# A transformer block with routed experts on one core: the experts' tiles begin at slot 5 of the last batch's step instead of slot 9

## The reference

```python
mod = (_silu(L0_c) @ L0_wmod).reshape(16, 6, 1, -1)
sa, ca, ga, sb, cb, gb = (mod[:, 0], ..., mod[:, 5])     # gates: |g| at least 0.25, sign kept
h = _layernorm(x) * (1 + ca) + sa
x = x + ga * attention(h)          # 16 heads of 8, rotary, causal, softmax, output projection
h = _layernorm(x) * (1 + cb) + sb
x = x + gb * ffn(h)
# ffn: logits = h @ router_w.T over 8 experts, the best 2 of each token, weights renormalised
#      expert e: gelu_tanh(h @ w_fc[e] + b_fc[e]) @ w_proj[e] + b_proj[e]   (128 -> 512 -> 128)
```

## Time and profile before

| | |
|---|---|
| median of 3 runs | 555.8 us (553.67 to 558.47) |
| the profiled execution | 555.56 us |
| its span, first to last instruction | 553.8 us |
| PE busy | 453.2 us (82% of the span) |
| DVE, POOL, ACT busy | 401.1, 346.9, 300.3 us |

### The profile page before, as it was taken

One profiled execution on the slowest core, in us unless ns is written; L12 is line 12 of the kernel. 1 busy time (PEld: TensorE's weight loads), 2 busy tenths in 40 slices (PEclk: granted clock), 3 DMA queues, 4 the chain that ended last, 5 costly groups with the idle time before them and its releaser, 6 DMA issues.

```text
span 553.8 us, 12554 instructions
## 1 busy us (share of the span) xinstructions
PE 453.2 (82%) x3543; PEld 334.8 (60%) x3543; DVE 401.1 (72%) x1194; ACT 300.3 (54%) x836; POOL 346.9 (63%) x483
## 2 busy tenths in 40 slices
PE   2567999889989889888988989689869679999940
PEld 1334556555655555555655655369859669999940
DVE  6757898899999799999999799635335424444763
ACT  1104565565555455555555555657647348878730
POOL 5655554556976856966966857825656554444872
PEclk9869999999999899999999999989999789999985
DMA  5145445635745725754745852422222322224723
GB/s 150 41 109 161 141 125 126 169 93 145 217 127 153 218 88 146 216 146 131 226 128 125 188 156 55 131 55 64 64 64 68 86 56 69 70 68 138 229 81 117
DMA packets 77731, 68.40 MB, mean 123 GB/s; under 512 B 10403, under 2 KB 71079, under 8 KB 77664
## 3 DMA queue, kind: packets, MB, share of 16 engines
q1 hardware_dynamic: 72160, 58.08, 38.3%
q0 software_dynamic: 4320, 8.47, 4.6%
q10 hardware_dynamic: 1184, 1.05, 0.6%
HBM read 25.98 MB, written 12.05 MB: 69 GB/s over the span
## 4 chain that ended last, share of the span: by engine, by line
PE 33%; DVE 31%; issue 11%; SPq 6%; DMA 5%; POOL 5%; another core or an unknown queue 4%; ACT 2%; DVEq 1%; POOLq 0%
DVE maxima L1379 10%; PE ps_sc L1545 8%; PE ps_max L1555 4%; PE ps_pv L1555 4%; DMA k_diags<-k_stacks 4%; PE misc L1706 3%; SPq L553 3%; PE ps_pv L1662 3%; DVE shifts L1393 2%; PE ps_max L1615 2%; DVE turned_b L1330 2%; DVE stats L978 2%; DVE z L993 2%; SPq L521 2%
## 5 line engine op out<-in xcount | busy, mean ns | idle before, releaser
L895 ACT ACTIVATE probs<-ps_sc 128x512 f32<-128x512 f32 x192 | 110.0, 596 | 79.6 <-PE ps_sc L1633 51.1
L1379 DVE TENSOR_REDUCE maxima<-ps_max 128x2 f32<-128x512 f32 (+1 forms) x192 | 130.5, 682 | 25.4 <-PE ps_max L1617 12.9
L749 POOL DMA_INDIRECT results<-after_k,after_e x71 | 70.1, 987 | 69.7 <-DVE after_k L1076 44.7
L759 POOL TENSOR_SCALAR_AFFINE_SELECT probs<-probs 128x512 f32<-128x512 f32 x128 | 82.1, 645 | 38.4 <-ACT probs L895 36.9
L1633 PE MATMUL ps_sc<-q_diags,k_stacks 128*128 128x512 f32 x192 | 96.5, 504 | 6.1 <-ACT probs L895 4.8
L1545 PE MATMUL ps_sc<-x_in,after_k 128*128 128x128 f32 x568 | 79.9, 286 | 18.5 <-ACT x_in L865 8.7
L859 ACT ACTIVATE after_k<-ps_sc,after_k 128x128 f32<-128x128 f32 x284 | 89.5, 373 | 0.3 <-PE ps_sc L1545 0.3
L1545 PEld LDWEIGHTS ps_sc<-x_in,after_k 128*128 128x128 f32 x568 | 72.5, 200 | 19.9 <-ACT x_in L865 13.8
L709 POOL DMA_INDIRECT sorted_rows<-rows,slots x64 | 65.4, 1022 | 14.5 <-issue 10.0
L1615 PE MATMUL ps_max<-k_diags,q_stacks 128*128 128x512 f32 x128 | 62.3, 486 | 0.7 <-DVE maxima L1379 0.7
L1662 PE MATMUL ps_pv<-probs,v_wides 128*32 128x256 f32 (+1 forms) x1024 | 56.2, 338 | 1.3 <-POOL probs L759 1.3
(11 more groups left out here) (181 smaller groups left out, 877.0 us busy)
## 6 DMA issues: line engine op xcount, KB each, us to landing
k_diags<-k_stacks SPq DMA_DIRECT2D x64, 128.0 KB
q_diags<-q_stacks SPq DMA_DIRECT2D x64, 128.0 KB
gate_now<-gate_rows SPq DMA_DIRECT2D x16, 320.0 KB
after_e<-sorted_rows SPq DMA_DIRECT2D x71, 65.0 KB
k_stacks<-high SPq DMA_DIRECT2D x32, 128.0 KB
q_stacks<-high SPq DMA_DIRECT2D x32, 128.0 KB
x_in<-in_x SPq DMA_DIRECT2D x16, 128.0 KB
k_stacks<-low SPq DMA_DIRECT2D x16, 128.0 KB
```

What stands on the lines that cost most here:

```text
L749: nc.gpsimd.indirect_dma_start(result_dram, bass.IndirectOffsetOnAxis(ap=row_in[m % RING][:, D + 1:D + 2].bitcast(U32), axis=0), y_out[m % ...
L759: nc.gpsimd.affine_select(four, four, [[0, 4], [1, P]], ALU.is_ge, 0.0, base=0, channel_multiplier=-1).then_inc(S["causal_done"], 1)
L895: nc.scalar.activation(probs[:, g % 2, c], ps_sc[u % 2][:], ACT.Exp, scale=SCALE).then_inc(S["exp_done"], 1)
L1379: nc.vector.tensor_reduce(to, of, AX, ALU.max).then_inc(S["max_done"], 1)
```

## The change

Edits that belong together:

- `TILES_AT` is 5: `first_tile` stands at the end of slot 4 of step 16 and tile 0 in slot 5, so 19 tiles lie in the steps and 52 in the loop. All that is counted from `TILES_IN` moves four tiles on.
- up goes to `misc2` and `ps_max1`; down goes to `misc0` for tiles 0 to 4 and to `ps_sc` from tile 5 on, since the scores of the last batch still use `ps_sc` until slot 7.
- The scaled biases `y_bias` get their own 3 x 128 floats instead of lying in `x_in` and `x_res`, and ACT no longer waits for the residual of batch 14 ahead of its first tile.
- PE waits for other things ahead of the first tile, of tiles 1 to 5, and of the last transposes of heads.
- DVE's first staging waits for the maxima instead of the scores of the last batch.
- The eight sorts of the first group's last pair are all in step 15 (slots 2, 3, 4, 5, 7, 8, 9, 10).

```diff
-TILES_AT = 9
+TILES_AT = 5
+Y_SPARE = 5
 TILES_IN = 2 * UNITS - TILES_AT
 SORT_AT = {2: (0, 0), 3: (0, 1), 5: (0, 2), 6: (0, 3), 9: (1, 0), 11: (1, 1)}
 SORT_LATER_AT = {0: (1, 2), 2: (1, 3)}
+SORT_CLOSE_AT = {2: (0, 0), 3: (0, 1), 4: (0, 2), 5: (0, 3), 7: (1, 0), 8: (1, 1), 9: (1, 2), 10: (1, 3)}
-        y_bias = [x_in[1][:, 0, :], x_in[1][:, 1, :], x_res[0][:, 0, :]]
+        y_bias_all = next_free(3 * D).rearrange("p (n d) -> p n d", n=3)
+        y_bias = [y_bias_all[:, n] for n in range(3)]
-        ps_y = [ps_max[1], ps_pv]
+        up_bank = [misc[2], ps_max[1]]
         def y_bank(m):
-            return ps_y[0] if m < 2 else ps_y[m % 2]
+            return misc[0] if m < Y_SPARE else ps_sc[m % 2]
-                    if s.sorts() and s.t < B and n in SORT_AT:
+                    if s.sorts() and s.t < B - 1 and n in SORT_AT:
                         sort_some(s, *SORT_AT[n])
-                    if s.routes() and s.t <= B and n in SORT_LATER_AT and s.pair >= 1:
+                    if s.t == B - 1 and n in SORT_CLOSE_AT:
+                        sort_some(s, *SORT_CLOSE_AT[n])
+                    if s.routes() and s.t < B and n in SORT_LATER_AT and s.pair >= 1:
                         sort_last(s, *SORT_LATER_AT[n])
-                    nc.scalar.activation(act[m % 2][:, hc, :], ps_sc[m % 2][:, hc * P:(hc + 1) * P], ACT.Gelu_apprx_tanh,
+                    nc.scalar.activation(act[m % 2][:, hc, :], up_bank[m % 2][:, hc * P:(hc + 1) * P], ACT.Gelu_apprx_tanh,
                         act_e.wait_ge(S["z_done"], 2 * B)
-                        act_e.wait_ge(S["x1_done"], B - 1)
             def first_tile():      # DVE
-                dve.wait_ge(S["score_mm"], UNITS * B)
+                dve.wait_ge(S["max_done"], UNITS * B)
             def tile(m):           # PE
-                if m in (1, 2):
+                if 1 <= m < Y_SPARE:
                     pe.wait_ge(S["y_done"], m)
-                if m == 3:
-                    pe.wait_ge(S["heads_done"], B * 4)
+                if m == Y_SPARE:
+                    pe.wait_ge(S["exp_done"], B * UNITS)
             def first_tile():      # PE
-                pe.wait_ge(S["exp_done"], B * UNITS)
+                pe.wait_ge(S["shift_out"], B * 4)
+                pe.wait_ge(S["attn_t_done"], B - 1)
                     elif name[:5] == "heads":
                         s.wait(pe, S["heads_done"], -1, 4, 4)
+                        if s.t == B and a == 0:
+                            pe.wait_ge(S["y_done"], Y_SPARE)
```

More of the change, by code:

```diff
@@ L1544, in up @@
                 for hc in range(HC):
-                    last = nc.tensor.matmul(ps_sc[m % 2][:, hc * P:(hc + 1) * P], staged[m % 3][:, hc * P:(hc + 1) * P],
+                    last = nc.tensor.matmul(up_bank[m % 2][:, hc * P:(hc + 1) * P], staged[m % 3][:, hc * P:(hc + 1) * P],
                                             row_t[m % 2], start=True, stop=True)
```

## The result

The change makes the kernel slower. The median went from 554.3 us (10 runs, 548.8 to 558.5) to 561.6 us (10 runs, 557.0 to 568.8), on the same chip; the ratio of undisturbed runs is 1.0105, with a 95% interval of 1.0075 to 1.0136. The profiled execution took 562.78 us (its span 561.0) against 555.56. So the loss is 7.2 us by the profiles, 7.3 by the medians and 5.8 by the ratio; 7.6 was forecast.

What follows compares the result with a forecast made beforehand. PE was busiest (82%), with about 4 us idle before the tiles; ACT's loads would bind the new slots. y(6) 15.5 us later less 7.9 for four tiles gave 7.6 slower: 555.56 + 7.6 = 563.2, likeliest 563.3, range 555.5 to 568.5.

Steps and rivals of the forecast that it cites:

- The loads hide: Rival for the four tile slots: table loads hide, only serial order stays; 2.4 us slower, 558; chance 0.20.
- PE sets the pace: Rival: PE, not ACT, paces the four tile slots, filling its idle 4 us; 4.2 us faster, 551; chance 0.15.
- the emptied pipe: Rival mechanism: each table switch also empties ACT's pipe, some 1.4 us more on seven switches, 573; chance 0.02.
- The earlier start: Before tile 0: staging directly follows the second norm's statistics, saving 4.4 us; y(0) at 365.35 instead of 368.98, 3.6 ahead.
- One of the signs of being wrong: At the first tile: the forecast is wrong if the first turn waits for rows (sorts not done by 353 us).
- Slots 5 to 8: Step 16, a tile each, table loads on ACT's chain: slot 6 takes 5.2 us, slot 7 5.25, slot 8 5.05.
- Slot 9: Step 16, weighing, router, rank, up and down: taken as 3.7 us, putting y(4) at 384.5.
- partly at the low clock: Reading of the 4.4 us that weighing to down took before, for which 3.7 us was taken.
- a rival (PE half idle, the clock down): Much slower: PE works 3.3 of 5.2 us in the four slots, clock at 1.2 GHz; about 4.5 us more, 568; case's chance 0.07.
- The unnamed waits: ACT's waits without a named releaser, 16.3 us in four pieces between 380 and 456 us; kept, 3 us either way.
- another sign that came true: Between 380 and 456 us: the forecast is wrong if waits without a named releaser change by more than 3 us.
- In time by 2.7 us, so 0: Load of tile 41, after the second group's last sort: in time for turn(41) by 2.7 us, so no cost.

Runs made afterwards that it cites:

- two sorts per tile: Changed kernel with the last pair's eight sorts two each behind tiles 26 to 29, instead of tiles 26 to 33: 547.8 us, ratio 1.0207.
- one pair of loads less: Changed kernel with the routing gap's exponential in step 16 on POOL as a power of e, 6 table loads instead of 8: 560.4 us, ratio 1.0118.
- both causes away: Changed kernel with exponentials instead of gelus in tiles 0 to 3 and the last pair's sorts two to a tile: 536.5 us, ratio 1.0004.
- the kernel that begins at slot 8: Changed kernel with tiles from slot 8 of step 16 instead of slot 5, 2 table loads: 557.2 us, ratio 1.0086.

## Why the prediction was right, and where it was not

- **Direction, size, mechanism.** 7.6 us slower was forecast through six loads on the chain from scores to down. The loads are there, at 1283 ns, four slots have the forecast length, and without the loads the loss is gone, while two loads elsewhere show no cost. "The loads hide" falls by the distances, "PE sets the pace" by ACT's 10.20 busy of 10.30 us, the emptied pipe by ACT's rows. The closeness of the sum, 563.3 against 561.6 us, is in part luck, as the points below say, and it holds for the first chip alone.
- **The earlier start.** Forecast 3.6 us for y(0), measured 3.7, though by other parts: up(0) took 1.13 us and the scores followed it at once, so the gelus ended 0.8 us sooner than forecast, but down(0) was at the low level, 2.07 us instead of 1.15. One of the signs of being wrong came true and did no harm: turn(0) waited 1.43 us for the rows. The last sort was early (348.34), but the first load was issued 5.1 us behind it, not 3.5. up(0) waited for the staged weights all the same, 1.09 us more.
- **Slots 5 to 8.** 5.2, 5.25, 5.05 forecast; 5.1, 5.1, 4.9 measured.
- **Slot 9 was mis-sized.** 3.7 forecast, 6.4 measured. The step that failed is the choice to have it "partly at the low clock": the row shows 0.50 for all of it. I had the cause in a rival (PE half idle, the clock down) but priced it in slots 5 to 8, where only down(0) suffered in this profile, and not behind them. That is why the place cost 9.6 us instead of 7.6 here. The 6.4 us are not a property of the change, though: the same distance is 4.1 us in the changed kernel on the second chip, 3.5 with two sorts per tile and 3.4 with one pair of loads less. In those the low level came sooner, in slots 7 and 8 (distances of 5.5 and 5.8, of 6.0, of 6.0). What the sum lacks is a stretch at the low level behind a waiting PE, and where it falls decides its price: the place cost 9.6, 8.9 and 6.3 us in the three profiles that have all the loads and no fillers.
- **The unnamed waits.** Kept as they were, 3 us either way. On the chain they fell by 10.7 us, against the 3 allowed, which is another sign that came true; yet the lateness fell only from 9.6 to 7.0 us over their stretch, and to 8.1 by the end. The statistics came 1.5 us earlier than in the profile before; in other profiles the kernel before has them at 355.41 us and the changed one at 354.64, so part of this is the execution's. 9.6 less 1.5 (from 9.6 to 8.1) less 1.5 for the statistics is 6.6, the span shows 7.2: the forecast is met because errors of opposite sign nearly cancel.
- **"In time by 2.7 us, so 0" for load 41** held in the first profile and not on the second chip, the only other one where the sorts stood as in the change. The step took the send of tile 33 and its sort as following y(33) at once, as in the profile before. With 2.4 us from y(33) to the sort that holds in the first profile; on the second chip it is 7.6 us, since POOL needs 2.6 to 2.8 us for a send and a sort, and PE 1.97 a tile. The kernel before has about the same lag on the two faster chips (6.2 and 6.8 us from y(29) to its send) and four tiles more until turn(41), which cover it. In the changed kernel it costs 16.2 - 12.0 = 4.2 us; with two sorts per tile that jump is gone. The wait at tile 24, 1.3 us with both causes away and 12.0 - 8.9 = 3.1 us without, comes from the same queue, where the gap's exponential stands behind sends and sorts; no run took that one away alone.
- **Open.** What makes the unnamed waits, present in all profiles on chips at 554 us and in none at 535. I read them as slack that lets POOL catch up: in the first profile the send of tile 33 begins 1.1 us after y(33), on the second chip 6.3, and where they are, load 41 is in time. No run took them away, so that is only argued. Open too: what the low clock and the order each cost in the kernel that begins at slot 8, 0.6 us or more of its loss, and why one pair of loads less shows in the distances and not in the time.

## What to carry to other kernels

Before work is interleaved on ScalarE, list the function tables in the order of its stream: here each change of table cost about 1.3 us or more where a chain went through it and nothing that shows where the engine idled, so the place decides, and not the count. When an edit brings a consumer closer to its producer, recompute the producer's queue by its own pace per item (here 2.6 us on POOL against 1.97 on PE) and not from one late event. Where an edit leaves TensorE waiting, price some of the work behind the waits at the low level, and try an early start together with filler matmuls; measure on more than one chip where waits without a named releaser appear.

## What the runs showed of the hardware

- The same kernel takes 554 us on one chip and 535 us on two others. Most of it is waits without a releaser: 19.8 us on the chain of waits in the first profile, none in that of the third chip, whose span is 21.8 us shorter. The same change was 1.0105 on the first and 1.0343 on the second.
- A load of the activation table takes 1283 ns with 0.01 to 0.02 us around it, in every profile, idle or busy.
- After PE was busy 5.08 of 10.30 us its granted clock was 0.50 for the next 6.5 us, in which it was busy throughout. Where such a stretch falls differs between executions of the same order (slot 7, 8 or 9 here). Eighteen useless matmuls gave back 4.7 us by the medians; with eleven, an early start went from 0.9998 to 0.9965.
- An indirect DMA takes POOL 0.96 to 1.25 us here with 0.3 us ahead of it, and 5.2 us passed from the start of the last sort to the turn of its rows on PE.
